# An end in two column parts with unread matmuls, and a layer norm moved from VectorE to ScalarE, in a sparse attention and sine/cosine layer

## The chip, the cores and the metric

One core of one Trainium2 chip runs the kernel. The metric is the device time of one execution in microseconds (us); lower is better.

## What is computed

The input x has 8 batches of 100 rows and 512 columns, the context 8 batches of 722 rows and 512 columns. The reference, cut to what matters:

```python
def _layernorm(x): return (x - mean(x)) / sqrt(var(x) + 1e-5)      # over the columns

def attention(q, k, v):                   # 16 heads of 32
    scores = einsum('bhqd,bhkd->bhqk', q @ Wq + bq, k @ Wk + bk) * 32 ** -0.5
    out = einsum('bhqk,bhkd->bhqd', sparsemax(scores), v @ Wv + bv)
    return out @ Wo + bo

def ffn(x):
    real = x @ cos(theta + theta_noise)
    imag = x @ sin(phi + phi_noise)
    return sqrt(real * real + imag * imag)

x = x + attention(_layernorm(x), ctx, ctx)
x = x + ffn(_layernorm(x))
```

## The kernel before, in words

The work goes by batches b and, in each, by two halves of 8 heads, so there are 16 half batches i = 2b and 2b + 1. Every engine runs the same list of phases, `PHASES` from -1 to 17, written out by hand. In phase i VectorE looks at the scores of half batch i (`maxes` takes 16 MAX8 of each head, L972, and `thresholds` finds the sparsemax thresholds, L980 to L1008). Meanwhile TensorE attends half batch i - 1 and makes the scores of half batch i + 1 (`scores`, L564). An even phase also makes the second half of the keys of batch b (`k_of(b, 2, ..)`, `k_of(b, 3, ..)`, L469) and its values (`v_of`, L469). An odd phase makes the first half of the keys of batch b + 1, its queries (`xT_of`, `q_of`) and the last projections of batch b - 1 (`x2T_of`, `ffn_of`, L537).

The orders around the change are these.

- TensorE's key, value, query and projection results go through the PSUM tensor `ring1`, three banks in turn (`slot1`): the fourth result waits until ScalarE has read the first (`one_read`). Scores and attention go through `ring2`, two slots in turn.
- ScalarE reads each key result twice, `ks` (L713) and `k_f` (L717), for GpSimd's `low_k` (L352) and for SyncE's `stack_k` (L259, L263), which copies the keys into `kst`. The scores of the first four heads wait for one such stack, those of the last four for the next (L564). In an even phase the order on ScalarE is `k_of(b,2,0)`, `k_of(b,2,1)`, `k_of(b,3,0)`, `k_of(b,3,1)`, a root of an earlier batch, `v_of(b,0)` and so on. Each `v_of(b,kc)` is followed by `high_ctx(b+1,kc)`, after which GpSimd does `low_ctx` (L344).
- In phase 0 (`b` = 0) ScalarE's first instructions are `k_of(0,3,0)` and `k_of(0,3,1)`, just after `whole_turns(1, wsin)` (L736, L739) of phase -1. SyncE's order there is `stack_k(0,2)`, `load_ctx(1,3)` (which waits for GpSimd's `low_ctx(1,0)`), `stack_k(0,3)`.
- Phase 1 ends on ScalarE with the two sine activations of the weights (L895), and phase 2 begins behind them. The square root lies in another activation table than the sine.
- The first layer norm of batch b + 1 is done in phase 2b: VectorE takes mean and variance (`ln1_stats`, L948 and L950) after head 4, ScalarE the root of the variance (`ln_sd`, L782) after five attention steps, VectorE inverts it and normalises `xq` in place at the end of the phase (`ln1_apply`, L954 and L956). TensorE's `xT_of` in phase 2b + 1 and GpSimd's last three `low_ctx` of phase 2b wait for that (`xn_ready`). The second layer norm runs in the same way in odd phases (`ln2_stats`, `ln2_apply`), with its root on ScalarE behind the four key results.
- GpSimd splits the thresholds for TensorE (`split_tau`, behind the first two `low_k` of a phase). TensorE's attention (L606) waits for it and for `verified`, which VectorE raises in `settle` after head 4 of the next phase. Where a check of the thresholds fails, `settle` first refines a head (`refine`, L1049 and on).
- The end: the last output projection (L520), `last_x` (L1118), the layer norm (L948, L950, L782, L954, L956), four transposes (L493), their copy (L705), the cosine and the sine projection, each of four matmuls of 512 columns (L537), two squares (L795), `last_y` (sum L1122, sum with x1 L1125) around `root` (L799), and the store of 200 KB (L267). Each f32 matmul stands in the trace as two records.

Of the kernel before, what the change touches and what calls it, by code (L numbers as in the profile page):

```python
# [46 lines left out]
def build_kernel(nc, x, ctx_in, Wq, bq, Wk, bk, Wv, bv, Wo, bo, theta, phi, theta_noise, phi_noise, out):  # L47
# [8 lines left out]
    NP = CK * KC  # L56
    HALF = N // 2
# [62 lines left out]
    with es:  # L120
# [50 lines left out]
        st2, mv2, sd2 = sb("st2", [L, 6]), sb("mv2", [L, 2]), sb("sd2", [L, 2])  # L171
        relu_row = dif[:, :, :].rearrange("p g n -> p (g n)")[:, 0:N]
# [12 lines left out]
        ring2 = es.enter_context(nc.psum_tensor("ring2", [P, 2, 2, 512], F32))  # L185
        ring1 = es.enter_context(nc.psum_tensor("ring1", [P, 3, 512], F32))
# [22 lines left out]
        ln1_stat, ln1_sd, xn_ready = sem("ln1_stat"), sem("ln1_sd"), sem("xn_ready")  # L209
        ln2_stat, ln2_sd, x2n_ready = sem("ln2_stat"), sem("ln2_sd"), sem("x2n_ready")  # L210
        res_ready, x1_ready, sqsum_ready, root_ready, y_ready = (
# [15 lines left out]
        def _(sp):  # L227
# [88 lines left out]
            store(B - 1)  # L316
            sp.wait_ge(stored, 16 * B)

        @block.gpsimd
        def _(pool):  # L320
# [90 lines left out]
            for i in PHASES:  # L411
                b, odd = divmod(i, 2)
                attended = 0 <= i - 1 < NH
                if odd:
                    if b + 1 < B:
                        low_k(b + 1, 0, 0)
                        low_k(b + 1, 1, 0)
                    if attended:
                        split_tau(i - 1)
                    if b + 1 < B:  # L420
                        low_k(b + 1, 0, 1)
                        low_k(b + 1, 1, 1)
                        if b + 1 > 0:
                            low_q(b + 1)
                    if b < 0:
                        fours()
                    if 0 <= b - 1 < B - 1:
                        sum_squares(b - 1)
                else:
                    if b < B:  # L430
                        low_k(b, 2, 0)
                        low_k(b, 2, 1)
                    if attended:
                        split_tau(i - 1)
# [12 lines left out]
                    if 0 < b < B:  # L447
                        attended_x(b - 1)

        @block.tensor  # L450
        def _(pe):
# [73 lines left out]
            def x2T_of(b):  # L525
                pe.wait_ge(x2n_ready, b + 1)
                transpose_x(("x2T", b), x2n)
                yield

            def ffn_of(b):  # L530
                if b == 0:
                    pe.wait_ge(ffn_w, 2)
                pe.wait_ge(one_read, seen1(("x2T", b)))
                for n, w in enumerate((wcos, wsin)):
                    psum = slot1(("ffn", b, n))[0:L, :]
                    for c in range(DC):
                        last = nc.tensor.matmul(psum, x2T[:, c, :], w[:, c, :], start=(c == 0), stop=(c == DC - 1))  # L537
                        if c == DC - 1:
                            last.then_inc(one_full, 1)
                        yield  # L540
# [154 lines left out]
        def _(act):  # L695
# [87 lines left out]

            def x2T_of(b):
# [4 lines left out]
            def square(b, n):  # L789
# [5 lines left out]
                nc.scalar.activation(sq[:, n, :], src, ACT.Square).then_inc(one_read, 1)  # L795
# [53 lines left out]
            for i in PHASES:  # L849
# [3 lines left out]
                if odd:  # L853
# [35 lines left out]
                    if 0 <= b - 1 < B:  # L889
                        square(b - 1, 1)  # L890
# [5 lines left out]
                else:  # L896
                    if 0 < b < B:
                        k_of(b, 2, 0)
                        k_of(b, 2, 1)
# [13 lines left out]
                    if b + 1 < B:  # L913
                        ln_sd(b + 1, mv1, sd1, ln1_stat, ln1_sd)
# [12 lines left out]
                    if b == 0:  # L927
                        for kc in range(3, KC):
                            v_of(b, kc)
                    if 0 < b < B:  # L930
                        o_of(b - 1)
            root(B - 1)

        @block.vector
        def _(dve):
# [184 lines left out]
            def last_y():  # L1120
                dve.wait_ge(one_read, seen1(("ffn", B - 1, 1)))
                nc.vector.tensor_tensor(sq[:, 1, :], sq[:, 0, :], sq[:, 1, :], ALU.add).then_inc(sqsum_ready, 1)  # L1122
                dve.wait_ge(root_ready, B)
                dve.wait_ge(stored, 16 * (B - 1))
                nc.vector.tensor_tensor(att[:, :], x1[:, :], sq[:, 0, :], ALU.add).then_inc(y_ready, 1)  # L1125
# [60 lines left out]
            for i in range(NH):  # L1186
                b, odd = divmod(i, 2)
                for h in range(HH):
# [9 lines left out]
                    if h == 4 and not odd and b + 1 < B:  # L1198
                        ln1_stats(b + 1)
# [3 lines left out]
                if not odd and b + 1 < B:  # L1203
                    ln1_apply(b + 1)
# [4 lines left out]
            ln2_apply(B - 1)  # L1209
# [26 lines left out]
```

## Time and profile before

| what | value |
|---|---|
| median of three runs | 655.63 us (655.6 to 660.14) |
| the profiled execution, its own time | 656.24 us |
| span of its trace | 654.5 us |
| busy TensorE, VectorE, ScalarE, GpSimd | 86%, 87%, 58%, 28% of the span |
| mean granted TensorE clock | 0.927 of full |

Busy time is the union of the recorded instructions of an engine. TensorE's weight loads (PEld) overlap its matmuls and are counted apart. Times in the rows are microseconds from the start of the span; in brackets stands how long the engine had been idle before the first instruction of the row and what ended that.

### The profile page before, as it was taken

What the parts mean: (1) busy time and instruction counts of PE and PEld (TensorE: products, weight loads), DVE (VectorE), ACT (ScalarE), POOL (GpSimd) and SP (SyncE); (2) the same over time, 40 slices, a digit from 0 to 9 for tenths busy, and PEclk for the clock granted to TensorE, in tenths of its full rate; (3) what the DMA queues carried; (4) which work ended last, traced back from release to release, by engine and by line L of the source; (5) the groups of instructions that cost most, each with busy time, mean ns of one, the idle gap of its engine ahead of it and who ended that gap; (6) DMA issues with size and microseconds to landing.
All of it is one profiled execution on the core that took longest, in us unless ns stands there. A gap on an engine that the chain in (4) does not pass through costs nothing.

```text
span 654.5 us, 14483 instructions
## 1 busy us (share of the span) xinstructions
PE 564.9 (86%) x4648; PEld 333.9 (51%) x4648; DVE 567.2 (87%) x2903; ACT 376.8 (58%) x656; POOL 180.5 (28%) x236
## 2 busy tenths in 40 slices
PE   2796999989921999999999999994599999996975
PEld 1353666635511655565656555652356655664442
DVE  5599999997976998999999999996799989999911
ACT  3585569656710567666676667662276757663241
POOL 2712521333130142234323241424005250501020
PEclk9877989979965999999999999998699999997698
DMA  9853122302230102240233113311302102110000
GB/s 307 285 167 99 31 65 70 80 31 57 87 91 4 32 1 65 91 113 3 55 92 92 31 47 96 89 41 40 100 2 75 55 24 61 54 29 15 1 15 13
DMA packets 33505, 44.25 MB, mean 68 GB/s; under 512 B 8385, under 2 KB 26817, under 8 KB 33414
## 3 DMA queue, kind: packets, MB, share of 16 engines
q1 hardware_dynamic: 32332, 41.16, 22.0%
q10 hardware_dynamic: 1088, 2.10, 0.9%
q8 instruction: 37, 0.61, 0.4%
q14 instruction: 48, 0.39, 0.2%
HBM read 23.77 MB, written 1.64 MB: 39 GB/s over the span
## 4 chain that ended last, share of the span: by engine, by line
PE 69%; issue 15%; ACT 7%; DMA 3%; SPq 3%; DVE 1%; POOL 1%; POOLq 0%; ACTq 0%; DVEq 0%
PE ring L469 32%; PE ring L537 8%; PE ring L618 6%; PE mix_bank L589 6%; PE ring L564 5%; PE ring L507 4%; PE ring L520 4%; ACT S L705 2%; SPq L259 1%; DMA ctx_f<-in_ctx 1%; PE ring L575 1%; ACT v L705 1%; DMA S<-in_L_xattn_Wk 1%; PE mix_bank L550 1%; ACT ctx L705 1%
## 5 line engine op out<-in xcount | busy, mean ns | idle before, releaser
L972 DVE MAX8 cand<-S 100x8 f32<-100x45 f32 (+1 forms) x2048 | 223.6, 196 | 2.1 <-issue 0.4
L469 PE MATMUL ring<-wv,ctx 128*121 128x512 f16 x576 | 154.6, 390 | 0.3 <-ACT v L705 0.3
L469 PE MATMUL ring<-ctx,wk 128*128 128x361 f16 x768 | 129.2, 325 | 5.1 <-DVE ctx L1156 4.6
L830 ACT ACTIVATE pT<-ring 121x800 f32<-121x800 f32 x96 | 80.5, 839 | 70.0 <-PE ring L618 69.4
L705 ACT ACTIVATE S<-ring 100x722 f32<-100x722 f32 x128 | 96.0, 773 | 30.9 <-PE ring L564 30.8
L469 PEld LDWEIGHTS ring<-ctx,wk 128*128 128x128 f16 x768 | 75.3, 100 | 50.7 <-issue 7.9
L344 POOL TENSOR_TENSOR ctx<-ctx_f,ctx 128x484 f16<-128x484 f32 x42 | 48.4, 1154 | 153.7 <-ACT ctx L705 82.9
L469 PEld LDWEIGHTS ring<-wv,ctx 128*121 128x121 f16 x576 | 71.8, 137 | 34.5 <-issue 7.5
L352 POOL TENSOR_TENSOR ks<-k_f,ks 128x361 f16<-128x361 f32 x64 | 56.6, 885 | 67.2 <-ACT k_f L717 63.7
L564 PE MATMUL ring<-kst,qst 96*100 96x361 f16 x256 | 63.5, 336 | 10.2 <-DMA kst<-ks 6.7
L618 PEld LDWEIGHTS ring<-qst,kst 99*121 99x121 f16 x768 | 57.3, 142 | 28.5 <-issue 14.0
L713 ACT ACTIVATE ks<-ring,bk_c 128x361 f16<-128x361 f32 x64 | 36.0, 562 | 56.9 <-PE ring L469 56.8
L618 PE MATMUL ring<-qst,kst 99*121 99x100 f16 x768 | 62.0, 226 | 1.8 <-ACT qst L705 1.8
L564 PEld LDWEIGHTS ring<-kst,qst 96*100 96x100 f16 x256 | 30.7, 130 | 51.1 <-issue 22.9
L589 PE MATMUL mix_bank<-pT,v 121*32 121x100 f32 x1536 | 54.9, 263 | 2.0 <-ACT aT L813 1.2
L705 ACT ACTIVATE qst<-ring 96x800 f16<-96x800 f32 (+1 forms) x32 | 25.7, 829 | 48.5 <-PE ring L606 45.4
L986 DVE TENSOR_TENSOR dif<-cand,tau 100x256 f32<-100x256 f32 (+1 forms) x64 | 50.6, 791 | 2.2
L606 PE MATMUL ring<-ident,tt 100*3 100x100 f16 x128 | 9.2, 221 | 48.2 <-issue 46.7
L589 PEld LDWEIGHTS mix_bank<-pT,v 121*32 121x32 f32 x1536 | 33.1, 112 | 33.3 <-issue 29.1
L995 DVE TENSOR_REDUCE f_sum<-dif 100x8 f32<-100x256 f32 (+1 forms) x64 | 49.7, 777 | 0.0
L989 DVE TENSOR_SCALAR over<-dif 100x256 bf16<-100x256 f32 (+1 forms) x64 | 36.9, 576 | 2.2
L705 ACT ACTIVATE v<-ring 121x256 f32<-121x256 f32 x96 | 31.4, 384 | 10.6 <-PE ring L469 10.6
(127 smaller groups left out, 692.9 us busy)
## 6 DMA issues: line engine op xcount, KB each, us to landing
kst<-ks SPq DMA_DIRECT2D x384, 45.1 KB, 1.9
ctx_f<-in_ctx SPq DMA_DIRECT2D x45, 242.0 KB, 2.9
xq<-in_x SPq DMA_DIRECT2D x8, 200.0 KB
xr<-in_x SPq DMA_DIRECT2D x8, 200.0 KB
out_y<-att SPq DMA_DIRECT2D x8, 200.0 KB
S<-in_L_xattn_Wk ACTq DMA_DIRECT2D x1, 1024.0 KB, 6.8
wq<-in_L_xattn_Wq ACTq DMA_DIRECT2D x1, 1024.0 KB, 11.4
wcos<-in_L_ffn_theta SPq DMA_DIRECT2D x1, 1024.0 KB, 10.4
```

The source lines that it names most:

```text
L344: pool.tensor_tensor(ctx2[:, 1, :, at], ctx_f[:, n % 3, :, :], ctx2[:, 0, :, at], ALU.subtract).then_inc(ctx_lo_ready, 1)
L352: pool.tensor_tensor(ks[:, n % 2, 1, at], k_f[:, u % 2, :], ks[:, n % 2, 0, at], ALU.subtract).then_inc(k_lo_ready, 1)
L469: last = nc.tensor.matmul(psum, lhs(c, i), w(c, j), start=(c == 0 and n == 0), stop=(c == DC - 1 and n == 2))
L537: last = nc.tensor.matmul(psum, x2T[:, c, :], w[:, c, :], start=(c == 0), stop=(c == DC - 1))
L564: last = nc.tensor.matmul(psum[0:L, half, 0:HALF], qst[0:3 * DH, b % 2, HH * part + h, :], kst[0:3 * DH, i % 3, h, half * HALF:(half + 1) ...
L589: last = nc.tensor.matmul(mix_ps[DH * j:DH * (j + 1), :], v[0:CK, i % 3, kc, DH * (G * g + j):DH * (G * g + j + 1)], pT[0:CK, st_unit(i, g ...
L618: last = nc.tensor.matmul(psum[0:CK, c, j * L:(j + 1) * L], kst[0:99, i % 3, G * g + j, kc * CK:(kc + 1) * CK], qst[0:99, b % 2, HH * part ...
L705: return nc.scalar.activation(dst, src, ACT.Copy, **kw)
L830: nc.scalar.activation(pT[0:CK, u % 3, :, :], src, ACT.Relu).then_inc(two_read, 1)
L972: last = nc.vector.max(pieces[:, h, :, n], S[0:L, HH * (i % 2) + h, cuts[n]:cuts[n + 1]])
L986: n = counted(nc.vector.tensor_tensor(dif[:, :, 0:E], cand[:, :, 0:E], t3.broadcast_to([L, HH, E]), ALU.subtract))
L995: counted(nc.vector.reduce_sum(f_sum[:, :], dif[:, :, 0:E], AX))
```

## The change

The first layer norm of batches 1 to 7 goes to ScalarE. `centre_x(b + 1)` runs in phase 2b behind `k_of(b,2,0)` (in phase 0: first of all): a Copy with a sum makes minus the mean, an Identity subtracts it in place, a Square with a sum makes the variance times 512, and Sqrt makes the root. Each waits for the one before it. VectorE inverts the root after head 6 of that phase and waits for it there. `scale_x(b + 1)` multiplies on ScalarE at the end of the phase, ahead of `o_of`. `ln1_stats`, `ln_sd` and `ln1_apply` of these batches are gone. GpSimd's wait for `xn_ready` becomes one for `flag_ready` of the same phase.

At the end, TensorE issues nine matmuls that nobody reads (f16, 128x512) before it waits for the last normalised rows, and two before it waits for their transposed copy. The last rows are only centred (`last_norm`); the inverted root becomes the `scale` of the squares. The sine projection runs in two halves of 256 columns, and the square, the sum, the root, the last sum and the store run for each half.

```diff
@@ sync
-            store(B - 1)
-            sp.wait_ge(stored, 16 * B)
+            for n, at in enumerate(LAST_HALVES):
+                sp.wait_ge(y_ready, B + n)
+                sp.dma_start(out[B - 1, :, at], att[:, at]).then_inc(stored, 16)
+            sp.wait_ge(stored, 16 * (B + 1))
@@ gpsimd, even phases, before low_ctx(b + 1, KC // 2)
-                                pool.wait_ge(xn_ready, b + 2)
+                                pool.wait_ge(flag_ready, 2 * b + 1)
@@ tensor
             def x2T_of(b):
+                if b == B - 1:
+                    pe.wait_ge(two_read, len(two))
+                    keep_warm(9)
                 pe.wait_ge(x2n_ready, b + 1)
...
             def ffn_of(b):
...
+                if b == B - 1:
+                    keep_warm(2)
                 pe.wait_ge(one_read, seen1(("x2T", b)))
                 for n, w in enumerate((wcos, wsin)):
                     psum = slot1(("ffn", b, n))[0:L, :]
-                    for c in range(DC):
-                        last = nc.tensor.matmul(psum, x2T[:, c, :], w[:, c, :], start=(c == 0), stop=(c == DC - 1))
...
+                    for at in (LAST_HALVES if b == B - 1 and n == 1 else (slice(0, D),)):
+                        if at.start:
+                            psum = last_sine[0:L, :]
+                        for c in range(DC):
+                            last = nc.tensor.matmul(psum[:, 0:at.stop - at.start], x2T[:, c, :], w[:, c, at],
+                                                    start=(c == 0), stop=(c == DC - 1))
...
+            def keep_warm(n):
+                for _ in range(n):
+                    nc.tensor.matmul(unread_bank[0:L, :], ctx2[:, 0, 0, 0:L], ctx2[:, 0, 1, 0:D], start=True, stop=True)
@@ scalar
+            def centre_x(b):
+                act.wait_ge(in_xq, 16 * (b + 1))
+                nc.scalar.activation(unread[:, :], xq[:, :], ACT.Copy, scale=-1.0 / D, accum_out=mv1[:, 0:1]).then_inc(ln_step, 1)
+                act.wait_ge(ln_step, 3 * b - 2)
+                nc.scalar.activation(xq[:, :], xq[:, :], ACT.Identity, bias=mv1[:, 0:1]).then_inc(ln_step, 1)
+                act.wait_ge(ln_step, 3 * b - 1)
+                nc.scalar.activation(unread[:, :], xq[:, :], ACT.Square, accum_out=mv1[:, 1:2]).then_inc(ln_step, 1)
+                act.wait_ge(ln_step, 3 * b)
+                nc.scalar.activation(sd1[:, 0:1], mv1[:, 1:2], ACT.Sqrt, bias=eps_t[:, :], scale=1.0 / D).then_inc(ln1_sd, 1)
+
+            def scale_x(b):
+                act.wait_ge(ln1_inv, b)
+                nc.scalar.activation(xq[:, :], xq[:, :], ACT.Identity, scale=sd1[:, 1:2]).then_inc(xn_ready, 1)
...
+            def last_roots():
+                parts = ring1[0:L, one["ffn", B - 1, 1] % 3, 0:D // 2], last_sine[0:L, 0:D // 2]
+                for n, at in enumerate(LAST_HALVES):
+                    act.wait_ge(one_full, one["ffn", B - 1, 1] + 1 + n)
+                    nc.scalar.activation(sq[:, 1, at], parts[n], ACT.Square, scale=sd2[:, 1:2]).then_inc(one_read, 1)
+                    act.wait_ge(sqsum_ready, B + n)
+                    nc.scalar.activation(sq[:, 0, at], sq[:, 1, at], ACT.Sqrt).then_inc(root_ready, 1)
@@ scalar, even phases
                     if 0 < b < B:
                         k_of(b, 2, 0)
+                    if b + 1 < B:
+                        centre_x(b + 1)
+                    if 0 < b < B:
                         k_of(b, 2, 1)
...
-                    if b + 1 < B:
-                        ln_sd(b + 1, mv1, sd1, ln1_stat, ln1_sd)
...
+                    if b + 1 < B:
+                        scale_x(b + 1)
                     if 0 < b < B:
                         o_of(b - 1)
-            root(B - 1)
+            last_roots()
@@ vector
+            def last_norm():
+                dve.wait_ge(ln2_stat, B)
+                dve.wait_ge(root_ready, B - 1)
+                nc.vector.tensor_scalar(x2n, x1[:, :], mv2[:, 0:1], None, ALU.subtract).then_inc(x2n_ready, 1)
+                dve.wait_ge(ln2_sd, B)
+                nc.vector.reciprocal(sd2[:, 1:2], sd2[:, 0:1]).then_inc(last_inv, 1)
...
-                    if h == 4 and not odd and b + 1 < B:
-                        ln1_stats(b + 1)
+                    if h == 6 and not odd and b + 1 < B:
+                        dve.wait_ge(ln1_sd, b + 2)
+                        nc.vector.reciprocal(sd1[:, 1:2], sd1[:, 0:1]).then_inc(ln1_inv, 1)
...
-                if not odd and b + 1 < B:
-                    ln1_apply(b + 1)
```

## Rows read from the trace of the kernel before

**Rows 1.** The page, part 1: busy us of each engine, share of the span, instructions

```profile
PE 564.9 (86%) x4648; PEld 333.9 (51%) x4648; DVE 567.2 (87%) x2903; ACT 376.8 (58%) x656; POOL 180.5 (28%) x236
```

**Rows 2.** Busy time by window: us, busy by engine (count), TensorE clock, DMA share, GB/s

```profile
62.00:150.00 88.00, 83.36 (x670) 51.12 (x671) 84.66 (x457) 59.54 (x105) 29.21 (x36) 0.94 0.19 52
236.00:449.00 213.00, 211.84 (x1809) 125.74 (x1808) 203.53 (x1114) 139.74 (x253) 73.48 (x98) 1.00 0.22 63
536.00:622.00 86.00, 79.59 (x698) 47.53 (x697) 82.46 (x417) 45.94 (x78) 13.10 (x20) 0.88 0.13 34
```

**Rows 3.** Waits, all engines: who waited for whom, us in total, times, longest us

```profile
PE ring L606 <- issue: 46.7, 3, 26.2
...
DVE sd L954 <- ACT sd L782: 10.6, 7, 3.0
```

**Rows 4.** Timeline of VectorE around two ends of its waits for ScalarE

```profile
152.83 0.16 DVE L954 RECIPROCAL sd<-sd 100x1 f32<-100x1 f32 x1 [3.01 <-ACT sd L782]
...
536.24 0.16 DVE L954 RECIPROCAL sd<-sd 100x1 f32<-100x1 f32 x1 [2.61 <-ACT sd L782]
```

**Rows 5.** Timeline, all engines, 44 to 63 us (phase 0)

```profile
44.60 5.20 DVE L972 MAX8 cand<-S 100x8 f32<-100x45 f32 x48
48.31 0.55 ACT L713 ACTIVATE ks<-ring,bk_c 128x361 f16<-128x361 f32 x1
51.06 0.61 ACT L705 ACTIVATE ctx<-ctx_f 128x484 f16<-128x484 f32 x1 [0.31 <-DMA ctx_f<-in_ctx]
51.82 1.12 POOL L344 TENSOR_TENSOR ctx<-ctx_f,ctx 128x484 f16<-128x484 f32 x1 [0.29 <-ACT ctx L705]
52.97 0.35 SPq L238 DMA_DIRECT2D ctx_f<-in_ctx  x1
...
62.23 0.51 PE L564 MATMUL ring<-kst,qst 96*100 96x361 f16 x2 [0.55 <-DMA kst<-ks]
```

**Rows 6.** Timeline of ScalarE and TensorE, 111 to 122 us (phase 2)

```profile
111.12 0.56 ACT L713 ACTIVATE ks<-ring,bk_c 128x361 f16<-128x361 f32 x1
...
113.22 2.75 PE L469 MATMUL ring<-wv,ctx 128*121 128x512 f16 x12
...
120.28 1.28 ACT L782 ACT_TABLE_LOAD   x1
121.58 0.29 ACT L782 ACTIVATE sd<-mv,eps_t 100x1 f32<-100x1 f32 x1
```

**Rows 7.** Timeline of ScalarE and TensorE, 272 to 277 us (phase 6)

```profile
272.71 0.56 ACT L713 ACTIVATE ks<-ring,bk_c 128x361 f16<-128x361 f32 x1 [1.55 <-PE ring L469]
...
276.20 2.75 PE L469 MATMUL ring<-wv,ctx 128*121 128x512 f16 x12
```

**Rows 8.** Lines by form: count, busy us, mean ns of one, idle before

```profile
L705 ACT ACTIVATE v<-ring 121x256 f32<-121x256 f32 x96 | 31.4, 384 | 10.6 <-PE ring L469 10.6
...
L799 ACT ACTIVATE sq<-sq 100x512 f32<-100x512 f32 x8 | 5.0, 629 | 2.1 <-POOL sq L378 1.4 <-DVE sq L1122 0.8
...
L1026 DVE DVE_READ_ACCUMULATOR dif<-dif,delta,zero 100x1 f32 x6 | 0.5, 82 | 0.0
```

**Rows 9.** Timeline of the end, 634 to 652 us

```profile
634.73 1.10 PE L520 MATMUL ring<-wo,aT 128*100 128x512 f32 x2 [0.47 <-ACT aT L813]
...
637.32 0.18 DVE L950 BATCH_NORM_AGGREGATE mv<-st 100x2 f32<-100x6 f32 x1
...
638.13 0.55 DVE L956 TENSOR_SCALAR sq<-x,mv,sd 100x512 f32<-100x512 f32 x1
...
645.16 3.60 PE L537 MATMUL ring<-wsin,k_f 128*100 128x512 f32 x8
...
649.43 0.69 DVE L1122 TENSOR_TENSOR sq<-sq 100x512 f32<-100x512 f32 x1 [10.75 <-ACT sq L795]
...
650.82 0.69 DVE L1125 TENSOR_TENSOR att<-x,sq 100x512 f32<-100x512 f32 x1 [0.69 <-ACT sq L799]
```

**Rows 10.** Busy time by window, the end; columns as in rows 2

```profile
640.20:643.60 3.40, 3.40 (x5) 1.17 (x5) 0.00 (x0) 0.00 (x0) 0.00 (x0) 0.50 0.00 0
```

More of the change, by code:

```diff
@@ L56, in build_kernel @@
     NP = CK * KC
+    LAST_HALVES = (slice(0, D // 2), slice(D // 2, D))
     HALF = N // 2
@@ L171, in build_kernel @@
         st2, mv2, sd2 = sb("st2", [L, 6]), sb("mv2", [L, 2]), sb("sd2", [L, 2])
+        unread = sb("unread", [L, D], mybir.dt.uint8)
         relu_row = dif[:, :, :].rearrange("p g n -> p (g n)")[:, 0:N]
@@ L185, in build_kernel @@
         ring2 = es.enter_context(nc.psum_tensor("ring2", [P, 2, 2, 512], F32))
+        last_sine, unread_bank = ring2[:, 0, 0, :], ring2[:, 1, 1, :]
         ring1 = es.enter_context(nc.psum_tensor("ring1", [P, 3, 512], F32))
@@ L208, in build_kernel @@
         step, fix, check_step = sem("step"), sem("fix"), sem("check_step")
-        ln1_stat, ln1_sd, xn_ready = sem("ln1_stat"), sem("ln1_sd"), sem("xn_ready")
+        ln1_stat, ln1_sd, ln1_inv, xn_ready = (sem(n) for n in ("ln1_stat", "ln1_sd", "ln1_inv", "xn_ready"))
+        ln_step = sem("ln_step")
         ln2_stat, ln2_sd, x2n_ready = sem("ln2_stat"), sem("ln2_sd"), sem("x2n_ready")
+        last_inv = sem("last_inv")
         res_ready, x1_ready, sqsum_ready, root_ready, y_ready = (
@@ L535, in ffn_of @@
                     psum = slot1(("ffn", b, n))[0:L, :]
-                    for c in range(DC):
-                        last = nc.tensor.matmul(psum, x2T[:, c, :], w[:, c, :], start=(c == 0), stop=(c == DC - 1))
-                        if c == DC - 1:
-                            last.then_inc(one_full, 1)
-                        yield
+                    for at in (LAST_HALVES if b == B - 1 and n == 1 else (slice(0, D),)):
[4 more added lines that the diff above has]
+                                                    start=(c == 0), stop=(c == DC - 1))
+                            if c == DC - 1:
+                                last.then_inc(one_full, 1)
+                            yield
+            def keep_warm(n):
+                for _ in range(n):
+                    nc.tensor.matmul(unread_bank[0:L, :], ctx2[:, 0, 0, 0:L], ctx2[:, 0, 1, 0:D], start=True, stop=True)
             def sum_flags(i):
@@ L794, in square @@
                     act.wait_ge(y_ready, b)
-                nc.scalar.activation(sq[:, n, :], src, ACT.Square).then_inc(one_read, 1)
+                if b < B - 1:
+                    nc.scalar.activation(sq[:, n, :], src, ACT.Square).then_inc(one_read, 1)
+                else:
+                    act.wait_ge(last_inv, 1)
+                    nc.scalar.activation(sq[:, n, :], src, ACT.Square, scale=sd2[:, 1:2]).then_inc(one_read, 1)
+            def last_roots():
[5 more added lines that the diff above has]
+                    nc.scalar.activation(sq[:, 0, at], sq[:, 1, at], ACT.Sqrt).then_inc(root_ready, 1)
             def root(b):
@@ L888, in _ @@
                             k_of(0, 2, h // 4)
-                    if 0 <= b - 1 < B:
+                    if 0 <= b - 1 < B - 1:
                         square(b - 1, 1)
@@ L1120, in last_y @@
             def last_y():
[L1121 to L1125, printed above, removed]
+                for n, at in enumerate(LAST_HALVES):
+                    dve.wait_ge(one_read, seen1(("ffn", B - 1, 1)) + n)
+                    nc.vector.tensor_tensor(sq[:, 1, at], sq[:, 0, at], sq[:, 1, at], ALU.add).then_inc(sqsum_ready, 1)
+                    dve.wait_ge(root_ready, B + n)
+                    dve.wait_ge(stored, 16 * (B - 1))
+                    nc.vector.tensor_tensor(att[:, at], x1[:, at], sq[:, 0, at], ALU.add).then_inc(y_ready, 1)
+            def last_norm():
[4 more added lines that the diff above has]
+                nc.vector.reciprocal(sd2[:, 1:2], sd2[:, 0:1]).then_inc(last_inv, 1)
             def ln2_apply(b):
@@ L1208, in _ @@
             ln2_stats(B - 1)
-            ln2_apply(B - 1)
+            last_norm()
             last_y()
```

## The prediction

> **What bounds the kernel now.** I read the busy shares first, then the windows, the waits, and the timeline at the places that the change touches. The shares decide nothing: TensorE and VectorE are both busy for 86 to 87% [rows 1]. By windows, TensorE is busy for 211.84 of the 213 us from 236 to 449, at full clock, VectorE for 203.53 [rows 2]. So in the long middle TensorE is full and VectorE has some room. The waits say the same. VectorE's wait for ScalarE's root of the second layer norm comes 7 times, 10.6 us in all [rows 3], and ends at 152.83 after 3.01 us idle and at 536.24 after 2.61 us [rows 4]. That root stands on ScalarE behind key results that TensorE makes, so at these points VectorE is early and TensorE with ScalarE sets its time. TensorE in turn waits long only three times, 46.7 us in all, each time for thresholds [rows 3]: twice while a head is refined, once late. From 536.24 to 622 VectorE is busy for 82.46 of 86 us and TensorE for less [rows 2]; this stretch hangs on VectorE, and the change takes nothing out of it, since no first layer norm is left there. Behind it comes a serial end.
>
> I conclude that work taken off VectorE before 536 is worth nothing unless TensorE or ScalarE gets earlier, that work added to ScalarE costs what it holds TensorE up, and that the end is worth what it is shortened by.
>
> **The layer norm on ScalarE: what goes.** Seven times VectorE loses mean and variance (about 0.9 us) and the normalisation (about 0.6 us), some 10 us in all. It lies where VectorE then waits anyway [rows 4], so I cost the gain at nothing, and at 1 us at best for the three long waits of TensorE, of which two end with a refinement on VectorE [rows 3].
>
> **What one `centre_x` costs.** Three passes over 100x512 at 0.629 us each, by the root of that shape [rows 8], are 1.89 us. The small root takes 0.29 [rows 6]. The trace shows no sum on ScalarE. VectorE's read of an accumulator takes 0.08 us [rows 8]; the two sums cost between nothing and a whole further pass each, 0 to 1.3 us. I take twice 0.08, as the nearest row, and 0.03 to 0.05 us for each of four handoffs. That makes 2.5 us, from 2.3 to 3.7.
>
> *Steady even phases (phases 4 to 12).* In phase 6 ScalarE idles 1.55 us before the second key result [rows 7]. So 2.5 us in that place delays this result by 1.0 us, the next by little and the fourth not at all. TensorE needs the bank of the second result at 276.20 [rows 7]. It was read at 273.7, and now at 274.7: covered by 1.5 us. GpSimd's split of the thresholds comes as much later and is needed by TensorE only some 2.6 us after it, behind the first value. `scale_x` (0.63 us) falls into ScalarE's wait for the output projection. Cost 0. If one `centre_x` took over 4.0 us, each such phase would pay the excess.
>
> *Phase 0.* Here ScalarE has no idle time: the third key result's reading starts at 48.31, right behind the previous pass [rows 5]. `centre_x(1)` comes ahead of it, so both key results, the first value and the context pass at 51.06 are 2.5 us later, less the 0.31 that this pass waits for its DMA: 2.2 us. Behind it hang, in turn, GpSimd's L344 (51.82 for 1.12, to 52.94), and SyncE's load at 52.97, which waits for just that, and behind the load in SyncE's queue the copies of the last key stack [rows 5]. TensorE already waits 0.55 us for them at 62.23 [rows 5], so there is no cover: +2.2 us for TensorE. From 62 to 150 it is busy for 83.36 of 88 us, part of it at half clock [rows 2], and I see no wait for VectorE in which the delay could vanish. VectorE itself now waits after head 6 of phase 0, from about 47 to 51. Its eight heads ended at 49.80 [rows 5], and now at 53.0: 3.2 us late, of which about 2.6 come back by phase 3 (no normalisation in phases 0 and 2, no statistics in phase 2). The rest is covered by the 3.01 us it waits at 152.83 [rows 4], which move later with TensorE.
>
> *Phase 2.* ScalarE is late here, behind the two sines. `centre_x(2)` comes ahead of the pass at 111.12 [rows 6], and holds the first square root after the sine, so the table load of 1.28 us moves here from 120.28 [rows 6]. The second key result is read 3.8 us later, at 115.9 instead of 112.1. TensorE's first value needs that bank and starts at 113.2 [rows 6]: it waits to 115.9, +2.7 us. What is saved at 120.28 (1.28 + 0.29) is no gain: TensorE is not waiting for ScalarE there.
>
> A page of the Trainium skill makes this dearer: ScalarE: Activation LUTs, section "What ACT_TABLE_LOAD costs", says that every switch of the set costs a drain of about 1.38 us beside the load. Here the root starts at 121.58, 0.02 us behind the load that began at 120.28 and took 1.28 [rows 6], so no drain is seen. With it phase 2 would cost 1.4 us more and the result would be 658.5; I go by the row.
>
> Sum of the middle: +2.2 + 2.7 = +4.9 us, carried on through the wait at 152.83. Bounds: 0 (both hidden) to +9 (each `centre_x` 3.7 us, and half clock for 3.4 us more behind the new stalls, 1.7).
>
> **The end: what goes.** The root and its inverse leave the path between the mean (done at 637.50) and the normalised rows (begun at 638.13) [rows 9]: -0.60 us, one handoff left. From the end of the sine projection (645.16 + 3.60 = 648.76) to the last sum (650.82 + 0.69 = 651.51) it takes 2.75 us [rows 9]. In halves, ScalarE's passes are 0.38 us (256 columns [rows 8]) and VectorE's half of 0.69, 0.35 [rows 9]; four of them and four handoffs of 0.03 are 1.6 us: -1.15, and the first half lies beside the second half's matmuls. Between halving nothing and halving all fixed cost the term lies between 0 and -1.35. The clock: from 640.20 to 643.60 TensorE was granted 0.50, half of 2.4 GHz, and was busy all 3.40 us [rows 10]. Ahead of that it stood idle from 635.83 (634.73 + 1.10) to the transposes behind 638.68 [rows 9]. The nine unread matmuls fill this: twelve of their shape take 2.75 us [rows 6], nine 1.9 us, from 635.6 to 637.6, where the rows are ready at 638.1, so they are in nobody's way. Held at full clock the stretch takes 1.7 us: -1.7. Bounds 0 and -1.7. At half clock the nine would take 3.8 us and delay the transposes by 1.5. The store's issue and landing stay, and the second half's DMA starts with the last sum as before; 0, from -0.3 to +0.4. Sum of the end: -3.45 us, from -4 to 0.
>
> **Sum.** 656.24 (the profiled execution) + 4.9 - 3.45 = 657.7. That execution lies 0.6 us above the median of 655.63, so against the median I forecast **657.1 us**. About 1% (6.6 us) is what a measurement of this kernel can tell from no change: no change by that measure.
>
> **Rivals.** *A: the end's gain alone, 652.2.* The two early delays vanish before 152.83. For it: TensorE has some 4.6 us not busy from 62 to 150 [rows 2], and the half clock there may fall otherwise. Against: its waits there are for ScalarE, which is later still.
>
> *B: the steady phases pay too, and it is slower, about 665.* The mechanism is the sum on ScalarE: if each of its two sums costs one more pass and each handoff 0.3 us, `centre_x` takes about 5.0 us. It decides from 4.0 us on, where TensorE runs out of its third bank [rows 7]. Then four phases pay 1.0 each (phase 4 lies ahead of TensorE's longest wait, 26.2 us [rows 3], which hides it), and the early two 2.5 more each: 657.1 + 4 + 5 = 666, less where SyncE's queue hides some. Against: nothing else on ScalarE in this trace takes twice its length.
>
> *C: the clock falls in the end all the same, 658.8.* The unread matmuls don't hold it; 1.7 us stay. For: two of them before the projection may be too few. Against: TensorE would be idle for under 1 us at a time.
>
> *D: nothing is bound as I say in the middle and VectorE's 10 us count, 646.* Against: VectorE idles before its own waits [rows 4].
>
> **How the numbers follow.** Forecast 0.5, A 0.23, C 0.11, B 0.09, D 0.07. The range goes from A with an end of -4 (651.6) to the forecast with the early cost at its bound (657.1 + 4.1 = 661.2): **651.6 to 661.3 us**. Slower by over 1% is B (0.09), faster by over 1% is D and a little of A (0.09); within 1% the rest, 0.82.
>
> **What would show it.** Right: ScalarE's passes of `centre_x` at 48.4 and at 111.2, the latter with the table load; TensorE's wait at 62.23 grown to about 2.8 us and a new one of 2.7 us at 113; VectorE's wait at 152.83 ending near 157.7; no new TensorE wait in phases 6 to 12; VectorE's waits for the root each longer by about 1.5 us; in the end a granted clock of 1.00 throughout, and 1.6 us from the last sine matmul to the last sum. Wrong: the refinement's first wait of TensorE starting and ending as before (A), a wait of TensorE for a key result in each even phase (B), or a second stretch at 0.50 in the end (C).

## The result, and the profile after

The changed kernel takes 664.48 us at the median of 22 executions (660.09 to 668.74), the kernel before 661.89 in as many (655.42 to 665.09). The ratio on record is 1.0096, interval 1.0069 to 1.0123. Medians here and below are over all executions; the ratios leave out those that lie over 1.5% above the fastest of their kernel. So the change makes the kernel slower, clear of the noise. How much is less sure: the two medians differ by 2.6 us (0.4%), the two means by 4.3 us (0.7%), and the ratio says 1.0%; how the executions are weighted in it is not on record. The forecast was 657.1, 1.5 us more than before, in 651.6 to 661.3. The direction held. The time lies outside the range, above all because the median of 655.63 that it started from was low: 13 of the 22 executions of the kernel before lie above 660.

The profiled execution took 668.58 us with a span of 666.8, 12.3 us more than before. Where these 12.3 us arise shows best at fixed points of VectorE's and TensorE's work. The waits of the changed kernel, all engines (us in total, times, longest):

```profile
PE ring L627 <- issue: 46.6, 3, 26.2
...
DVE sd L1005 <- ACT sd L803: 15.0, 6, 3.1
...
DVE sd L1260 <- ACT sd L814: 5.3, 2, 3.5
```

TensorE's long waits for thresholds are as in [rows 3] (46.6 us, before 46.7). VectorE's wait for the second norm's root has grown from 10.6 to 15.0 us, and there are 5.3 us of new waits for the first norm's root: that is where its saved work went. The timeline of VectorE at the points of [rows 4]:

```profile
160.68 0.16 DVE L1005 RECIPROCAL sd<-sd 100x1 f32<-100x1 f32 x1 [3.06 <-ACT sd L803]
...
545.53 0.16 DVE L1005 RECIPROCAL sd<-sd 100x1 f32<-100x1 f32 x1 [2.84 <-ACT sd L803]
```

These are 7.85 us and 9.3 us later than before. So 7.9 us of the loss are there by 160 us, and in the next 385 us 1.4 us come to it. The timeline of phase 0, as in [rows 5]:

```profile
48.34 0.61 ACT L808 ACTIVATE unread<-xq 100x512 uint8<-100x512 f32 x1
48.86 0.19 ACT L808 ACTIVATION_READ_ACCUMULATOR unread<-xq 100x1 f32 x1
49.08 0.72 ACT L810 ACTIVATE xq<-xq,mv 100x512 f32<-100x512 f32 x1
49.83 0.63 ACT L812 ACTIVATE unread<-xq 100x512 uint8<-100x512 f32 x1
...
50.59 0.29 ACT L814 ACTIVATE sd<-mv,eps_t 100x1 f32<-100x1 f32 x1
50.79 0.54 ACT L734 ACTIVATE ks<-ring,bk_c 128x361 f16<-128x361 f32 x1
50.91 0.16 DVE L1260 RECIPROCAL sd<-sd 100x1 f32<-100x1 f32 x1 [3.45 <-ACT sd L814]
...
55.19 0.34 SPq L243 DMA_DIRECT2D ctx_f<-in_ctx  x1
...
64.42 0.84 PE L585 MATMUL ring<-kst,qst 96*100 96x361 f16 x2 [3.56 <-DMA kst<-ks]
```

`centre_x` takes 2.54 us from 48.34 to 50.88. The load that SyncE's last stack stands behind is issued 2.2 us later, and TensorE waits 3.56 us instead of 0.55 for the stack. The scores behind this wait start 2.2 us later than before (64.42 instead of 62.23); the wait grew by more than that because TensorE had reached it 0.8 us earlier. Then comes the clock. From these scores to a fixed point of the next attention TensorE has the same work in both kernels. This point in the kernel before, then in the changed one:

```profile
92.27 0.55 PE L589 MATMUL mix_bank<-pT,v 121*32 121x100 f32 x16 [1.20 <-ACT aT L813]
```

```profile
97.10 0.89 PE L610 MATMUL mix_bank<-pT,v 121*32 121x100 f32 x16 [1.20 <-ACT aT L861]
```

The way there took 30.0 us before and 32.7 now, 2.7 us more: behind the stall TensorE's granted clock was 0.51 from 63.0 to 69.9 us. Phase 2, as in [rows 6]:

```profile
119.64 1.28 ACT L814 ACT_TABLE_LOAD   x1
120.94 0.29 ACT L814 ACTIVATE sd<-mv,eps_t 100x1 f32<-100x1 f32 x1
121.14 0.54 ACT L734 ACTIVATE ks<-ring,bk_c 128x361 f16<-128x361 f32 x1
...
122.18 2.15 PE L476 MATMUL ring<-wv,ctx 128*121 128x512 f16 x9 [2.52 <-ACT k_f L738]
```

The table load stands there as forecast, again with the root 0.02 us behind its end, and TensorE's new wait is 2.52 us. A steady phase, as in [rows 7]:

```profile
282.33 0.54 ACT L734 ACTIVATE ks<-ring,bk_c 128x361 f16<-128x361 f32 x1
...
285.02 2.75 PE L476 MATMUL ring<-wv,ctx 128*121 128x512 f16 x12
```

TensorE started this phase's keys at 276.92 and begins on the value 8.1 us later, as before (268.10 and 276.20); it waits for nothing. Last, windows (columns as in [rows 2]): the start, the middle, the last attention and the projections behind it.

```profile
62.00:150.00 88.00, 78.54 (x616) 48.20 (x617) 82.48 (x423) 58.78 (x103) 23.36 (x31) 0.90 0.20 53
244.80:457.80 213.00, 211.83 (x1809) 125.73 (x1808) 197.42 (x1088) 148.37 (x272) 73.21 (x97) 1.00 0.23 63
...
633.80:651.60 17.80, 17.14 (x159) 10.97 (x160) 0.05 (x1) 6.53 (x9) 2.53 (x2) 0.50 0.05 12
...
653.60:664.00 10.40, 8.82 (x35) 4.80 (x33) 1.46 (x5) 2.91 (x6) 0.00 (x0) 1.00 0.02 6
```

The middle is full as before, with VectorE 6 us less busy. (Over the whole span VectorE's lines of the first norm lose 10.4 us, as forecast, but its busy time falls by 5.3 us only, from 567.2 to 561.9: others of its instructions took longer, and why is not shown.) The third row is the surprise. The last attention ran at half clock, 0.50, and took 17.8 us. In the profiled execution before it had been this:

```profile
625.00:635.90 10.90, 9.70 (x158) 6.07 (x158) 0.03 (x1) 6.31 (x9) 2.53 (x2) 1.00 0.08 22
```

That is 6.9 us of the 12.3, in a piece of the kernel that the change doesn't touch. The end itself:

```profile
649.48 2.03 PE L527 MATMUL ring<-wo,aT 128*100 128x512 f32 x2 [0.47 <-ACT aT L861]
651.30 3.21 PE L561 MATMUL ring<-ctx 128*100 128x512 f16 x9
651.55 0.69 DVE L1169 TENSOR_TENSOR x<-ring,xr 100x512 f32<-100x512 f32 x1 [19.11 <-PE ring L527]
...
653.22 0.49 DVE L1183 TENSOR_SCALAR sq<-x,mv 100x512 f32<-100x512 f32 x1
...
654.35 0.51 PE L500 MATMUL ring<-ident,sq 100*128 100x100 f32 x4
...
659.03 3.62 PE L552 MATMUL ring<-wsin,k_f 128*100 128x256 f32 x16
...
664.10 0.42 DVE L1177 TENSOR_TENSOR att<-x,sq 100x256 f32<-100x256 f32 x1 [0.48 <-ACT sq L843]
```

From the start of the first add (651.55) to the end of the last (664.52) it takes 13.0 us, before 15.6. From there to the end of the span it is 2.25 us, before 2.95. The nine unread matmuls began at half clock, took 3.21 us and held the transposes up to 654.35, though the rows were ready at 653.71: 0.6 us lost to the change's own filler.

### The profile page after: what moved, and what is told of

Same layout as the page of the kernel before. It is cut to its first block, busy times and chain, and to the rows that moved or that the text cites. A ratio compares the mean times of both kernels' runs of the same rounds, so it can differ in the third digit from the quotient of the medians.

```text
span 666.8 us, 14547 instructions
## 1 busy us (share of the span) xinstructions
PE 577.2 (87%) x4667; PEld 343.8 (52%) x4667; DVE 561.9 (84%) x2884; ACT 396.2 (59%) x700; POOL 180.7 (27%) x236
## 4 chain that ended last, share of the span: by engine, by line
PE 70%; issue 15%; ACT 9%; POOL 2%; DMA 2%; DVE 1%; SPq 1%; POOLq 0%; ACTq 0%; DVEq 0%
PE ring L476 31%; PE ring L552 7%; PE ring L639 7%; PE mix_bank L610 6%; PE ring L585 5%; PE ring L514 4%; PE ring L527 4%; ACT S L726 3%; PE ring L596 1%; ACT v L726 1%; PE mix_bank L571 1%; PE ring L627 1%; ACT ctx L726 1%; DMA bq<-bq 1%; PE ring L500 1%
## 5 line engine op out<-in xcount | busy, mean ns | idle before, releaser
L476 PE MATMUL ring<-wv,ctx 128*121 128x512 f16 x576 | 157.9, 396 | 2.9 <-ACT k_f L738 2.5
L639 PEld LDWEIGHTS ring<-qst,kst 99*121 99x121 f16 x768 | 60.8, 150 | 30.0 <-issue 15.2
L639 PE MATMUL ring<-qst,kst 99*121 99x100 f16 x768 | 65.5, 234 | 1.8 <-ACT qst L726 1.8
L610 PE MATMUL mix_bank<-pT,v 121*32 121x100 f32 x1536 | 57.6, 273 | 1.5 <-ACT aT L861 1.2
L1037 DVE TENSOR_TENSOR dif<-cand,tau 100x256 f32<-100x256 f32 (+1 forms) x64 | 52.0, 812 | 2.2
L610 PEld LDWEIGHTS mix_bank<-pT,v 121*32 121x32 f32 x1536 | 34.9, 117 | 33.7 <-issue 28.0
L627 PE MATMUL ring<-ident,tt 100*3 100x100 f16 x128 | 9.5, 226 | 47.7 <-issue 46.6
L1040 DVE TENSOR_SCALAR over<-dif 100x256 bf16<-100x256 f32 (+1 forms) x64 | 41.4, 647 | 2.2
L726 ACT ACTIVATE v<-ring 121x256 f32<-121x256 f32 x96 | 31.4, 384 | 10.6 <-PE ring L476 10.6
```

The costliest lines, as they stand in the source:

```text
L476: last = nc.tensor.matmul(psum, lhs(c, i), w(c, j), start=(c == 0 and n == 0), stop=(c == DC - 1 and n == 2))
L610: last = nc.tensor.matmul(mix_ps[DH * j:DH * (j + 1), :], v[0:CK, i % 3, kc, DH * (G * g + j):DH * (G * g + j + 1)], pT[0:CK, st_unit(i, g ...
L639: last = nc.tensor.matmul(psum[0:CK, c, j * L:(j + 1) * L], kst[0:99, i % 3, G * g + j, kc * CK:(kc + 1) * CK], qst[0:99, b % 2, HH * part ...
L726: return nc.scalar.activation(dst, src, ACT.Copy, **kw)
L1037: n = counted(nc.vector.tensor_tensor(dif[:, :, 0:E], cand[:, :, 0:E], t3.broadcast_to([L, HH, E]), ALU.subtract))
```

## The experiments

### Taking the change apart

Four kernels: the end alone; the layer norm on ScalarE alone; the whole but batches 1 and 2 normalised as before; the whole but batch 1 as before. The split is by a constant:

```diff
-                    if b + 1 < B:
+                    if LN_FROM <= b + 1 < B:
                         centre_x(b + 1)
```

(and the same for `scale_x`, the waits and VectorE's old instructions). Expected of the end alone, the norm alone, batches 3 to 7, batches 2 to 7:

> The new end alone, first layer norm as before. Theory (the layer norm costs only in phases 0 and 2, the end gives 3): 2.5 to 3.5 us faster than before, up to VectorE's first add of the end nothing moves by over 1 us apart from the half clock. Rival 1 (the changed kernel's loss comes from the last attention at half clock, which the new end itself brings on): 3 us or more slower than before, the last attention lasting 17 us instead of 11. Rival 2 (each steady even phase pays): says nothing of this kernel, as the theory.

> The layer norm of batches 1 to 7 on ScalarE alone, end as before. Theory: 7 to 10 us slower than before, of it 4.7 in two stalls of TensorE (at 62 and at 120 us) and 2 to 5 at half clock behind them, all of it there by 160 us. Rival 1: under 5 us slower. Rival 2: VectorE's wait for its root late in the kernel ends more than 10 us later than before, and the lag grows from phase to phase.

> The whole change, but batches 1 and 2 keep their layer norm on VectorE, so that phases 0 and 2 are as before. Theory: as the end alone, 2.5 to 3.5 us faster than before; both early stalls gone. Rival 1: no better than the changed kernel, within 2 us of it. Rival 2: some 3 us worse than the end alone, one part in each of phases 6 to 12.

> The whole change, but batch 1 keeps its layer norm on VectorE, so that phase 0 is as before and phase 2 is as changed (with the table load ahead of the second key result). Theory: about 2.5 to 4 us slower than the kernel with batches 1 and 2 on VectorE, and 2 to 5 us faster than the whole change; TensorE waits 0.6 us at 62 us and 2.5 us in phase 2. Rival 1: the stall of phase 2 makes no difference to the time.

| kernel | median us (executions) | ratio to before, 95% |
|---|---|---|
| before | 663.18 (29) | |
| end alone | 654.63 (6) | 0.986 (0.980 to 0.993) |
| norm alone | 669.30 (12) | 1.010 (1.006 to 1.013) |
| whole, norm from batch 3 | 657.41 (12) | 0.988 (0.984 to 0.992) |
| whole, norm from batch 2 | 661.24 (12) | 0.999 (0.996 to 1.002) |

The order is the theory's: the norm loses, and the end gains. The sizes are not. The end alone is 8.5 us faster at the median where 2.5 to 3.5 were expected, the norm alone 6.1 slower where 7 to 10 were, and the norm from batch 3 lies 2.8 above the end alone, so this table does not yet show that batches 3 to 7 cost nothing. The single executions show why. Those of the end alone lie at 650.9 to 652.8 and at 656.5 to 660.7, those of the kernel before at 654 to 655 and at 660 to 666. The mean granted clock of each execution is on record and goes with its time: in the kernel before 0.929 in the two at 654 and 655, and 0.912 to 0.915 in those at 664 to 666. The four profiled executions had the last attention at a mean clock of 0.50, 0.50, 0.58 and 0.60, in 15.8 to 17.7 us. So a second effect, as large as the whole change, lies over the measurement.

The profile of the norm alone also shows the early stalls by themselves. It has both of them (3.46 and 2.52 us), and in this execution the clock did not fall behind the first:

```profile
62.00:70.00 8.00, 6.10 (x31) 4.07 (x32) 7.69 (x16) 4.14 (x7) 1.56 (x2) 1.00 0.19 49
...
63.90 0.51 PE L578 MATMUL ring<-kst,qst 96*100 96x361 f16 x2 [3.46 <-DMA kst<-ks]
...
93.93 0.55 PE L603 MATMUL mix_bank<-pT,v 121*32 121x100 f32 x16 [1.20 <-ACT aT L850]
```

(the first line a window, with the columns of [rows 2]; the others TensorE's timeline). The way from the scores behind the stall to the fixed point took 30.0 us again, and VectorE's wait of [rows 4] ended at 156.64, 3.8 us later than before instead of 7.85. So the stall is there each time, and the half clock behind it is not.

### Holding the clock in the last attention

TensorE waits twice ahead of the last attention, 1.82 and 0.99 us in the changed kernel and 1.7 to 1.8 and 1.0 us in the four profiles above. In the one profile that had this attention at full clock, that of the kernel before, the first wait was only 0.40 us. I filled both waits with unread matmuls (operands and bank as in `keep_warm`):

```diff
+                    if i == NH:
+                        pe.wait_ge(two_read, two["tau", NH - 1])
+                        keep_warm(7)
                     if i > 0:
                         sum_flags(i - 1)
...
                     if b == B:
                         run(attended_o, 1)
+                        keep_warm(6)
```

Expected, in the kernel before, with the end alone, in the whole change, and with the norm from batch 3:

> The kernel before, with thirteen matmuls more that nobody reads, seven before TensorE's wait for the last thresholds' marks and six before its wait for the last split thresholds. Clock theory (the last attention runs at half clock in most runs, because TensorE waits some 2.8 us in two pieces ahead of it, and that sets the spread of the times): faster than before by 5 to 8 us at the median, the last attention in 11 us, the runs within 3 us of each other. Rival (the half clock comes from the sparse matmuls of the attention itself): no gain, half clock there all the same.

> The new end with the same thirteen matmuls. Clock theory: 2.5 to 4 us below the kernel before with them, near 651, all runs close together; so the new end is worth 3 us and what it showed beyond that was the clock. Rival (the new end itself keeps the clock better): little gain over the new end alone in its good runs, but 7 us or more below the kernel before with them.

> The whole change with the same thirteen matmuls. Theory of the early stalls: slower than the new end with them by 5 to 8 us (4.7 in two stalls, the rest half clock behind them), and about 659 to 661. If the change's loss were the last attention's clock, it would lie within 1.5 us of the new end with them.

> The change without the layer norms of batches 1 and 2 on ScalarE, with the same thirteen matmuls. Theory: within 1.5 us of the new end with them, since the steady phases cost nothing. Rival (each steady phase pays): 2 us or more slower than that.

| with the thirteen matmuls | median us | all executions | ratio to before without them, 95% |
|---|---|---|---|
| before | 657.17 (12) | 653.6 to 658.9 | 0.996 (0.993 to 1.000) |
| end alone | 653.23 (6) | 651.7 to 655.0 | 0.990 (0.984 to 0.996) |
| whole change | 659.60 (12) | 655.8 to 661.3 | 0.999 (0.996 to 1.003) |
| whole, norm from batch 3 | 653.46 (12) | 652.1 to 654.7 | 0.991 (0.988 to 0.995) |
| before, without them, same chip | 660.29 (29) | 654.5 to 663.7 | |

The window of the last attention, whole change:

```profile
633.90:644.90 11.00, 9.87 (x161) 6.42 (x161) 0.07 (x1) 6.31 (x9) 2.40 (x2) 1.00 0.07 20
```

Full clock and 11.0 us, against 17.8 without them. All twelve kernels of this document with the thirteen matmuls had 1.00 in the last attention of their profile, in 10.8 to 11.0 us; of the six without them, one had. The clock theory holds; the rival, that the sparse matmuls of the attention lower the clock, falls. In the kernel before, the gain is 3.1 us at the median rather than the expected 5 to 8, and the spread shrinks from 9 to 5 us, not to 3: this clock is not all of the spread. On this steadier ground the parts can be read: the end is worth 657.17 - 653.23 = 3.9 us, the norm from batch 3 on costs 0.2, that of batches 1 and 2 costs 659.60 - 653.46 = 6.1, and the whole change is 2.4 us slower (all five on one chip, in medians whose executions spread by 3 to 6 us).

### What the early part and the end consist of

All of these have the thirteen matmuls. They ran on another chip than the kernels above, and those of the next section on a third; the kernel before had medians of 660.29, 662.01 and 660.79 on the three, so a difference between two of these groups can be off by 1 to 2 us. The first two take the early part apart, the second by SyncE's order in phase 0; the last two the end.

```diff
+                    if b == 0:
+                        stack_k(b, 3)
                     if b + 1 < B:
                         load_ctx(b + 1, 3)
                     if b > 1:
                         store(b - 2)
-                    if b < B:
+                    if 0 < b < B:
                         stack_k(b, 3)
```

> The whole change but batch 1's layer norm on VectorE, with the thirteen matmuls ahead of the last attention. It splits the 6.4 us between the whole change (659.6) and the end alone (653.2), both with them: 2.5 to 3.5 us over the end alone if phase 2 costs its stall of 2.5 and no clock, so near 656; the other 3.5 would be phase 0's. If phase 2 costs nothing, near 653.5; if phase 0 costs nothing, near 659.5.

> The whole change with the thirteen matmuls, SyncE's order in phase 0 changed: the last key stack ahead of the context load that waits for GpSimd. Theory (phase 0's delay comes to TensorE through SyncE's queue, behind the load): TensorE's wait for the stack, 3.6 us at 61, shrinks to under 2 us and the kernel gains 2 to 4 us on the whole change with the thirteen matmuls. Rival (ScalarE's own lateness sets it, whatever the queue): the wait stays over 3 us and the time within 1 us.

```diff
-                if b == B - 1:
-                    pe.wait_ge(two_read, len(two))
-                    keep_warm(9)
...
-                if b == B - 1:
-                    keep_warm(2)
```

> The new end without its eleven unread matmuls, but with the thirteen ahead of the last attention, layer norm as before. Theory: the clock falls to half during the two last projections as in the kernel before, and the kernel is 1 to 2.5 us slower than with the eleven (653.2). Rival (the eleven do nothing): within 0.5 us.

```diff
-    LAST_HALVES = (slice(0, D // 2), slice(D // 2, D))
+    LAST_HALVES = (slice(0, D),)
```

> The new end with the sine projection, square, sum, root and store in one piece instead of two halves, else as the end with the thirteen matmuls. Theory: 1 to 1.8 us slower (1.15 by the forecast and some 0.4 to 0.9 of the store, which is half as large); from the last sine matmul to the last sum 2.7 us instead of 1.8.

Norm from batch 2: 656.66 us (12), 3.2 over the norm from batch 3 and 2.9 under the whole, both of the group before. So phases 2 and 0 cost about 3 us each. With SyncE's order changed the whole change takes 655.25 (12), 4.3 less, and TensorE waits

```profile
60.98 0.51 PE L587 MATMUL ring<-kst,qst 96*100 96x361 f16 x2 [1.01 <-DMA kst<-ks]
```

1.01 us for the last stack instead of 3.35 and starts 3.4 us earlier (60.98, not 64.34). `centre_x(1)` is as long and starts only 0.8 us earlier (47.51, not 48.27): the delay reached TensorE by the queue, since SyncE held the stack behind a load that waited for GpSimd. The rival falls. Of the 4.3 us, 2.3 are the shorter wait; in this trace the half clock behind it is gone, too.

Without its eleven unread matmuls the end takes 655.13 (12), 1.9 over the 653.23 with them, and its window has the half clock back:

```profile
637.60:644.40 6.80, 5.70 (x10) 2.48 (x11) 0.46 (x2) 0.70 (x2) 0.00 (x0) 0.50 0.00 0
```

In one piece instead of halves it takes 654.23 (12), 1.0 more, which across two chips is not clear of noise by itself. The traces say more: from the last sum to the end of the span it has 2.94 us, in halves 2.24, so the smaller store gives 0.7, and from the end of the last sine matmul to that of the last sum it takes 2.83, in halves 1.88.

### What was left, and a version that beats both

Two delays of 2.2 to 2.5 us do not make 6.1. The profile of the whole change with the thirteen matmuls shows, at 62 and at 97 us:

```profile
62.00:70.00 8.00, 5.66 (x16) 3.42 (x17) 7.69 (x17) 2.52 (x4) 1.07 (x1) 0.57 0.18 49
97.00:104.00 7.00, 6.96 (x78) 5.11 (x79) 6.76 (x14) 4.20 (x6) 0.36 (x1) 0.51 0.26 65
```

The end alone, with the same thirteen matmuls and no norm moved, shows in its windows

```profile
62.00:70.00 8.00, 8.00 (x41) 5.18 (x39) 7.83 (x11) 5.29 (x10) 4.08 (x2) 1.00 0.14 33
90.00:97.00 7.00, 5.80 (x87) 4.57 (x84) 6.69 (x18) 5.22 (x9) 1.16 (x1) 0.69 0.27 68
97.00:104.00 7.00, 7.00 (x32) 4.52 (x31) 6.73 (x22) 5.01 (x8) 0.00 (x0) 0.83 0.51 155
```

The half clock at 62 is new. That at 97 is not: over the 14 us from 90 to 104 both kernels have a mean of 0.76, and the end alone has its half clock 4.5 us earlier. Followed at TensorE's fixed points, the two executions part by 2.5 us at the last stack (61.80 and 64.34), by 2.7 more behind it, where the whole change has half clock from 63.0 to 69.8, and by 2.5 at the value of phase 2: 7.7 of the 7.9 us between their spans (651.6 and 659.5).

I filled the three early waits, too (22 unread matmuls ahead of the first scores of phase 0, 12 ahead of the fifth, 10 ahead of the first value of phase 2):

```diff
                 for h in heads:
+                    if i == 1 and h in (0, G):
+                        keep_early(22 if h == 0 else 12, ("s", 1, h))
                     if h % G == 0:
...
+                    if b == 1:
+                        keep_early(10, ("tau", 1))
                     run(fill, 4)
```

> The whole change with the thirteen matmuls, and 22, 12 and 10 unread matmuls in its three early waits (49 to 54, 61 to 64, 120 to 122 us). Theory (what phase 0 and 2 cost beyond their stalls is half clock behind them): 2 to 4 us under the whole change with the thirteen (659.6), no half clock from 51 to 70. Rival (only the stalls count): within 1 us of 659.6.

657.40 us (12), 2.2 under the 659.60 at the median; the ratios to the kernel before (1.000 and 0.999) do not show the gain, but in the trace VectorE's wait of [rows 4] ends at 157.56 instead of 160.63. Less clock is lost: at 50 to 62 us the mean is 1.00 instead of 0.72 (the kernel before has 0.72 there, too, so this half clock is not of the change's making), and behind the stall at 63 us the half clock lasts 3.4 us instead of 6.8, where none was expected:

```profile
62.00:70.00 8.00, 6.66 (x26) 4.18 (x27) 7.69 (x16) 3.87 (x7) 0.00 (x0) 0.79 0.17 45
97.00:104.00 7.00, 5.87 (x52) 3.89 (x50) 6.69 (x15) 5.52 (x11) 0.00 (x0) 1.00 0.31 73
```

Then the same means without the norm on ScalarE (h1: end, thirteen matmuls, SyncE's order; h2: with 22 and 2 early matmuls), and with the norm from batch 3 on top of that (h4):

> The new end with the thirteen matmuls and SyncE's order of phase 0 changed, layer norm on VectorE. Theory: the 1 to 1.6 us that TensorE waits at 61 for the last key stack go, so 1 to 2 us under the same without it (653.2). Rival (something else binds there): within 0.5 us.

> The same with 22 unread matmuls in TensorE's 5 us wait for the first scores of phase 0 and two in the next. Theory (the half clock from about 51 to 58 comes from that wait): no half clock there, 1.5 to 3 us less than without them. Rival (the matmuls delay the scores, or the clock falls all the same): no gain, or a loss.

> As the kernel with the end, the queue and the early matmuls, and the layer norms of batches 3 to 7 on ScalarE. Theory (VectorE's time is worth nothing, ScalarE's is free there): within 0.7 us of the one without them. Rival (VectorE's 7 us less count once the rest is tighter): 1 us or more faster.

| kernel | median us | ratio to before, 95% |
|---|---|---|
| h1 | 651.79 (6) | 0.990 (0.984 to 0.996) |
| h2 | 652.42 (12) | 0.990 (0.986 to 0.993) |
| h4 | 652.51 (12) | 0.991 (0.988 to 0.995) |
| before, same chip | 660.79 (29) | |

With SyncE's order the end with the thirteen matmuls is 1.4 us lower at the median than without it (653.23). That is not shown to be a gain: the ratios are 0.990 both, the six executions of each overlap, and in the traces the wait for the stack shrinks from 1.63 to 0.36 us, but TensorE's scores behind it start at 61.70 instead of 61.80. The early filler gives nothing on top, where 1.5 to 3 us were expected, although its trace has no half clock from 50 to 62 us. The norm of batches 3 to 7 gives nothing either, as the theory said, though VectorE is busy for 6.7 us less (559.8 against 566.5). All three beat both the kernel before and the changed one; they can't be told apart. h1 is the simplest of them: the new end, the filled waits ahead of the last attention, SyncE's order, and no norm moved.

## Why the prediction was right or wrong

*What bounds the middle.* Right. Busy shares of 86 and 87% looked like a tie, and VectorE's waits told who leads: 10.4 us of its work were taken away, and its waits for the two roots grew by 9.7.

*One `centre_x` at 2.5 us, steady phases at 0.* Right: 2.54 us, and 0.2 us for five batches (653.46 against 653.23). The pieces were less right than their sum: the two reads of the accumulator took 0.19 each, not 0.08, and the handoffs next to nothing.

*Phase 0 at +2.2 and phase 2 at +2.7, sum +4.9.* The mechanism was right in both, and the sizes as well (2.2 us later at the last stack, 2.52 us of wait in phase 2). The term that failed is the clock behind the first, which the sum had at 0 and only the bound had at 1.7: the same work took 32.7 us instead of 30.0, so 2.7 us where the clock falls, and in one of the executions it didn't. At the medians the early part costs 6.1 to 6.4.

*The end at -3.45.* Nearly right in the sum, -3.9 at the medians. In the two traces with the thirteen matmuls its parts are: the root off the path 0.65 (0.60 forecast), the clock in the projections 1.44 (1.7), the halves up to the last sum 0.85 (1.15), the store 0.7 (forecast at 0). That the sum came out is in part luck: the store made up for the two that were smaller.

*Sum.* +1.45 forecast, +2.4 with the last attention's clock held in both, +2.6 between the medians without that.

*The step that failed most* is the first of the sum: "656.24 (the profiled execution) + 4.9 - 3.45", set against a median of three. The kernel before has 661.89 at the median of 22; that is 6.3 of the 7.4 us between 657.1 and 664.48. It took over the last attention at full clock, as the profile showed it. The trace had TensorE idle 1.50 us just ahead of that attention, and one of the three times was 660.14, and I asked what the idle time at 636 does to the clock, but not what that at 623 could do in another execution. Held on purpose, this clock is worth 3.1 us at the median to the kernel before; in the two profiled executions it made 6.9 us of the 12.3. What made up the rest of the 6.3 is not shown.

*The rivals.* A (the early delays vanish) fell with the norm alone at +1%, B with the steady phases, D with the norm from batch 3. C was aimed at the right cause in the wrong place: the clock that fell is the attention's, ahead of the unread matmuls; the projections behind them ran at 1.00.

*Open.* The ratio of 1.0096 is 6.4 us, the difference of the medians 2.6, with the clock held 2.4. Whether more of the changed kernel's executions have the last attention at half clock can't be said: the others show only a mean clock of the whole (0.913 to 0.930 in the changed kernel), not one by stretch.

## What to carry to other kernels

Work moved to an engine with idle time is free only in the phases in which that idle time stands in front of it; price the first phases, where the engine is still behind, by themselves, and follow the delay through the DMA queue's order, not only through the engines. Where a kernel's times spread by more than the change, look for short TensorE waits (here 1.8 and 1.0 us) ahead of a sparse serial stretch, and try filling them before comparing versions. Before a half-clock stretch is put down to the change, look for it in a kernel without the change. A profile is one execution: ask of each full-clock stretch in it what the clock would cost if it fell there.

## What the runs showed of the hardware

- The same attention of about 160 matmuls ran at 1.00 in 10.9 us in an execution of the kernel before and at 0.50 in 17.8 us in one of the changed kernel, after idle pieces of 0.40 and 1.50 us there and 1.82 and 0.99 us here. Thirteen unread 128x512 f16 matmuls in these pieces went with 1.00 in all twelve kernels profiled with them.
- The same stall of 3.5 us at 61 us was followed by half clock from 63.0 to 69.9 in the changed kernel and by full clock in the norm alone; the work behind it took 32.7 and 30.0 us.
- Unread matmuls cost when the clock is already low: nine took 3.21 us and delayed the next step by 0.6, where at full clock they took 2.11.
- On ScalarE a sum costs 0.19 us (ACTIVATION_READ_ACCUMULATOR) beside a pass that is no longer than without it (0.61 to 0.63 us for 100x512), and with a per-row bias or scale operand the pass took 0.72 and 0.73.
- A 100x256 pass from PSUM with a scale operand took 0.47 us where 100x512 took 0.69, and VectorE's 100x256 add 0.43 where 100x512 took 0.69: halves cost about two thirds.
- Storing the last 100x512 rows in two halves ended 0.7 us sooner after the last sum (2.24 against 2.94 us).
